# Splitting the node products of the second half into F32R parts, with three buffers in place of four

## The reference

```python
row, col = src, dst                      # edge_index[0], edge_index[1]
neighbor_sum = segment_sum(x[col], row)  # over the edges
deg = maximum(segment_sum(ones, row), 1)
mean_neighbor = neighbor_sum / deg[:, None]
h_mean = (x + mean_neighbor) * 0.5 @ W_mean + b_mean
h_concat = concatenate([x @ W_ego + b_ego, mean_neighbor @ W_nb + b_nb], axis=1)
gate = sigmoid(gate_weight * node_vec + gate_bias)[:, None]
x = layernorm(x + (1 - gate) * h_mean + gate * h_concat)
```

## Time and profile before

| | |
|---|---|
| median of 3 runs | 2863.28 us (2862.87 to 2864.31) |
| profiled execution, its own time | 2864.34 us |
| its span in the trace | 2862.5 us |
| mean granted TensorE clock | 0.973 of full speed |
| PE busy in the span | 2641.2 us (92%) |
| DVE / ACT / POOL busy | 2393.4 (84%) / 1851.0 (65%) / 1582.5 (55%) us |

### The profile page before, as it was taken

One profiled execution on the slowest core, in us unless ns is written; L12 is line 12 of the kernel. 1 busy time (PEld: TensorE's weight loads), 2 busy tenths in 40 slices (PEclk: granted clock), 3 DMA queues, 4 the chain that ended last, 5 costly groups with the idle time before them and its releaser, 6 DMA issues. The chain is left out here.

```text
span 2862.5 us, 53163 instructions
## 1 busy us (share of the span) xinstructions
PE 2641.2 (92%) x14009; PEld 1610.8 (56%) x14009; DVE 2393.4 (84%) x7769; ACT 1851.0 (65%) x3839; POOL 1582.5 (55%) x1491
## 2 busy tenths in 40 slices
PE   4699989999999499999999999999999999976774
PEld 2466668788887255555555555555555555543442
DVE  8888877777777688888888888888888888878996
ACT  2355555666665277777777777777777777757885
POOL 0476727777776555454545454545455555306776
PEclk9799999999999699999999999999999999989998
DMA  9899986666665587777777777777777777647894
GB/s 346 298 350 350 351 295 202 198 199 203 203 204 183 155 211 220 213 220 214 220 213 222 214 222 212 219 218 221 213 223 213 222 212 217 180 131 239 276 281 149
DMA packets 544668, 653.52 MB, mean 228 GB/s; under 512 B 244334, under 2 KB 451882, under 8 KB 544550
## 3 DMA queue, kind: packets, MB, share of 16 engines
q1 hardware_dynamic: 468518, 440.38, 52.2%
q0 software_dynamic: 69472, 208.99, 23.4%
q10 hardware_dynamic: 6560, 2.84, 0.4%
HBM read 315.65 MB, written 299.10 MB: 215 GB/s over the span
## 5 line engine op out<-in xcount | busy, mean ns | idle before, releaser
L1242 ACT ACTIVATE hidT<-bank,b1c 128x512 f32<-128x512 f32 x490 | 336.7, 687 | 414.3 <-PE bank L1532 340.4
L1151 POOL TENSOR_TENSOR u_hc<-u_hc 128x1536 f32<-128x1536 f32 x98 | 270.1, 2756 | 550.9 <-issue 429.4
L961 PE MATMUL bank<-w_node,xT 128*128 128x384 f32 x1564 | 558.6, 495 | 15.1 <-ACT bank L584 15.0
L1532 PE MATMUL bank<-xh,w1h 128*128 128x512 f16 x1568 | 469.2, 381 | 23.3 <-DMA xh<-eh 15.7
L1532 PE MATMUL bank<-xl,w1h 128*128 128x512 f16 x1568 | 468.2, 380 | 0.0
L1532 PE MATMUL bank<-xh,w1l 128*128 128x512 f16 x1568 | 468.2, 380 | 0.0
L584 ACT ACTIVATE bank<-bias_all 128x512 f32<-128x512 f32 x391 | 234.3, 599 | 235.7 <-DVE H L689 234.3
L961 PEld LDWEIGHTS bank<-w_node,xT 128*128 128x128 f32 x1564 | 288.5, 193 | 161.4 <-ACT bank L584 17.2
L1548 PE MATMUL bank<-hidT,w2f 128*64 128x256 f32 x3136 | 360.1, 382 | 0.8 <-ACT hidT L1242 0.8
L1373 DVE STREAM_TRANSPOSE feat<-catT 32x256 f32<-32x256 f32 x784 | 342.5, 437 | 17.0 <-ACT catT L1251 2.4
L1354 DVE TENSOR_SCALAR hidT<-bank,b1c 128x512 f32<-128x512 f32 x294 | 220.6, 750 | 120.7 <-PE bank L1532 112.3
(11 more groups left out here) (255 smaller groups left out, 5199.3 us busy)
## 6 DMA issues: line engine op xcount, KB each, us to landing
hc_tab<-H SPq DMA_DIRECT2D x78, 680.0 KB
er<-edge_tab SPq DMA_DIRECT2D x98, 512.0 KB, 4.4
X<-in_x SPq DMA_DIRECT2D x78, 640.0 KB, 5.2
h_row<-hc_tab SPq DMA_DIRECT2D x97, 512.0 KB
out_x<-o_row SPq DMA_DIRECT2D x97, 512.0 KB, 5.0
edge_tab<-u_x SPq DMA_DIRECT2D x98, 256.0 KB, 3.9
edge_tab<-feat SPq DMA_DIRECT2D x98, 256.0 KB
hc_tab<-zero_row SPq DMA_DIRECT2D x18, 1344.0 KB
```

The costliest lines, as they stand in the source:

```text
L961: ins = t_.matmul(p[:, 0:384], xT[t // 2 % XR][:, t % 2, c * P:(c + 1) * P], w_node[:, c, :], start=False, stop=c == 1, skip_group_check=True)
L1151: g.tensor_tensor(c, c, u_hc[s][:, :, MULT:MULT + 3].unsqueeze(3).to_broadcast([P, 4, 3, P]), ALU.mult).then_inc(u_scaled, 1)
L1242: a.activation(hidT[m][:, :], bank[2 + m % 2][:, :], ACT.Relu, bias=b1c[:, m:m + 1])\
L1532: ins = t_.matmul(bank[2 + m % 2][:, :], w[:, c, m * P:(m + 1) * P], xx[s][:, :, :].rearrange("p (k c) e -> p c k e", c=2)[:, c, :, :], st ...
```

## The change

From pair 92 (tile 184) on, a node pair is split as the edge sums are: ACT writes the rounded F32R copy to `xhigh`, DVE subtracts it from bank 0 into `xlow` (`low_x`, at odd steps, behind `add` and ahead of the other side work), and `product` issues six F32R matmuls with the split weights `w_nodeh`, `w_nodel`. PE's `turn` of the next pair then waits for `low_x`, not for ACT's copy. The buffers `xT` and `accT`/`accL` go from four to three; `xhigh` and `xlow` have three each. `DECODE` goes from step 16 to 20, the sums begin at step 184 and spread over 188 steps, and `PUT_LAG` goes from 13 to 29.

```diff
@@ weights
+        w_nodeh, w_nodel = sb("w_nodeh", [P, 2, 384], F32R), sb("w_nodel", [P, 2, 384], F32R)
...
                 st.done(v.tensor_copy(w_nbh[:, :, :], w_nb[:, :, :]))
-                st.wait()
+                st.done(v.tensor_copy(w_nodeh[:, :, :], w_node[:, :, :]))
+                st.wait()
+                st.done(v.tensor_tensor(w_nodel[:, :, :], w_node[:, :, :], w_nodeh[:, :, :].bitcast(F32),
+                                        ALU.subtract))
@@ buffers
-        XR = 4
+        XR = 3
         xT = [tmp(f"xT{b}", [P, 2, D]) for b in range(XR)]
+        XS = 3
+        xlow = [tmp(f"xlow{b}", [P, 2, D], F32R) for b in range(XS)]
+        xhigh = [tmp(f"xhigh{b}", [P, 2, D], F32R) for b in range(XS)]
+        x_low = sem("x_low")
...
-        AR = 4
+        AR = 3
@@ plan
-        PUT_LAG = 13
-        SORT, PHASES, DECODE, SUMS, SPAN, FIX = 0, 7, 16, 195, 177, 377
+        PUT_LAG = 29
+        SORT, PHASES, DECODE, SUMS, SPAN, FIX = 0, 7, 20, 184, 188, 377
+        SPLIT = SUMS // 2 // 1 * 1
+        SPLITS = tuple(range(SPLIT, NT // 2 + 1, 1))
+        def nth(p):
+            return (p - SPLIT) // 1
+        def in_parts(p):
+            return p in SPLITS
@@ ScalarE, copy_x
+                    to = xhigh[nth(p) % XS] if in_parts(p) else xT[p % XR]
@@ VectorE
+                def low_x(p):
+                    many = min(2, NT + 1 - 2 * p)
+                    dve.wait_ge(xt_copied, p + 1)
+                    if nth(p) >= XS:
+                        dve.wait_ge(p_ready, 2 * SPLITS[nth(p) - XS] + 2)
+                    q = nth(p) % XS
+                    v.tensor_tensor(xlow[q][:, 0:many, :],
+                                    bank[0][:, 0:many * D].rearrange("p (t d) -> p t d", t=many),
+                                    xhigh[q][:, 0:many, :].bitcast(F32), ALU.subtract).then_inc(x_low, 1)
...  in side(), behind decode, tables and shares, ahead of low_sum and run_sum
+                    if now % 2 == 1 and in_parts((now - 1 + LEAD_X) // 2):
+                        low_x((now - 1 + LEAD_X) // 2)
@@ TensorE, turn
-                    if p:
+                    if in_parts(p - 1):
+                        pe.wait_ge(x_low, nth(p - 1) + 1)
+                    elif p:
                         pe.wait_ge(xt_copied, p)
@@ TensorE, product
+                    pair = t // 2
+                    if in_parts(pair):
+                        pe.wait_ge(x_low, nth(pair) + 1)
+                        high, low = xhigh[nth(pair) % XS][:, t % 2, :], xlow[nth(pair) % XS][:, t % 2, :]
+                        n = 0
+                        for c in range(2):
+                            for part_, w in ((high, w_nodeh), (high, w_nodel), (low, w_nodeh)):
+                                n += 1
+                                ins = t_.matmul(p[:, 0:384], part_[:, c * P:(c + 1) * P], w[:, c, :], start=False,
+                                                stop=n == 6, skip_group_check=True)
+                        ins.then_inc(p_ready, 1)
+                        return
```

More of the change, by code:

```diff
@@ L575, in copy_x @@
                     many = min(2, NT + 1 - 2 * p)
-                    a.activation(xT[p % XR][:, 0:many, :], bank[0][:, 0:many * D].rearrange("p (t d) -> p t d", t=many),
+                    to = xhigh[nth(p) % XS] if in_parts(p) else xT[p % XR]
+                    a.activation(to[:, 0:many, :], bank[0][:, 0:many * D].rearrange("p (t d) -> p t d", t=many),
                                  ACT.Copy).then_inc(xt_copied, 1)
@@ L958, in product @@
                     p = bank[NODE[t % 3]]
-                    pe.wait_ge(xt_copied, t // 2 + 1)
+                    pair = t // 2
[10 more added lines that the diff above has]
+                        return
+                    pe.wait_ge(xt_copied, pair + 1)
                     for c in range(2):
```

## The result

| | before | after |
|---|---|---|
| median of 3 runs | 2863.28 us | 2893.21 us (2892.90 to 2893.98) |
| span of the profiled execution | 2862.5 us | 2892.2 us |
| mean granted TensorE clock | 0.973 | 0.972 |
| PE / DVE busy | 2641.2 / 2393.4 us | 2605.5 / 2450.4 us |

The changed kernel is slower: the ratio is 1.0101, with a 95% interval from 1.0087 to 1.0116. PE is busy 36 us less, and still the span is 29.7 us longer.

A forecast was written before the change was run, and what follows sets the result against it. TensorE was taken to set the pace at full clock, POOL nearly as full. Terms +15 + 4 - 6 + 1.5 + 7 = +21.5 us on 2864.34 gave 2885.8, forecast as 2885 us; range 2840 to 2902.

The forecast's parts named there:

- The wait: Before the next node turn, PE waits for low_x, queued on DVE behind the odd tile's three instructions: 1.21 us uncovered.
- One sign: Expected in the trace: POOL waits for acc in the blocks of steps where PE waits for low_x.
- 188 steps, +15: Node steps 185 to 372, with sums: 548 us where the same steps cost 533 before, so 15 us lost.
- Steps without sums, +4: Steps 181 to 184 and 375 to 390: same wait, two steps 3.84 instead of 3.02; 4 us lost, bounds 0 to 7.
- Decode, -6: Decode four steps later: four more tiles of 1.51 us fit into DVE's wait for the sorted edges; 6 us won.
- start, +1.5: Ahead of the stage: two more weight splits on DVE (0.56 and 0.96) with nothing beside them; 1.5 us lost.
- The start of the sums, +7: Steps 184 to 205: about 4 us waiting for first gathered rows, some 3 more at the cn ring; bounds 0 and 15.
- the POOL rival: Node stage: the wait is covered and POOL's gathers and scatters set the pace; about 2841 us, chance 0.15.
- Rings, 0: Three buffers in place of four in the rings of node pairs and sums cost nothing.
- A smaller wait: The turn's wait for low_x is near 0.8 us and cancels against the gain: 2855 to 2868 us, chance 0.14.
- The dearer hand-over: At step 205, clears drain slower beside earlier gathers and ACT stands 20 us longer: about 2905 us, chance 0.06.
- The clock rival: PE falls to half clock in steps with the uncovered wait: some 185 us more, 3070 us, chance 0.03.

The follow-up runs named there:

- the early clears: Table's last clears in two larger pieces behind tiles 184 and 189, not five: changed kernel 2875.09 us; kernel before with new decode, sums and lag, unsplit products, 2855.46 us.
- The plan alone: Kernel before with decode at step 20, sums from step 184 over 188 steps and put lag 29, products left in float32: 2868.78 us, ratio 1.0014.

## Why the prediction came out as it did

The sign and the mechanism were right, and one term of the sum was too small by more than half.

*The wait.* Forecast: about 1.2 us, some 50 times, released by DVE's write of `xlow`, in blocks set by the parity of the sums. The trace has exactly these blocks. Each link of the chain holds: DVE starts 0.20 behind the odd product (507.34 to 507.54), and from the end of that product's issue to L872 it is 1.94 us in the cycle shown, which is 1.31 without the gate copy (0.09) and the variances (0.54); 1.30 was forecast. The last link was shorter: L872 ends 0.06 ahead of the turn, where 0.15 was taken. There are 52 pauses in the whole stage, one of them the 7.58 at the start of the sums. The 43 of 470 to 930 us are 1.03 on average by the profile, which counts from the modelled end of a record, 0.34 behind its start where the next could have started after 0.175; with that difference 1.2. The run with `low_x` at the even step shows that it is this wait which costs: without it the time falls by 41 us. One sign came out only weakly: POOL was to wait for `acc` in the blocks, and from 470 to 930 us it waits 4.7 us for it, but 25.7 us for ACT's `cn`.

*188 steps, +15.* Two steps take 5.08 where 5.17 was forecast, and 6.33 on the mean of the five cycles from 497.12 to 528.75 where 6.29 was forecast. With these, 44 x 5.08 + 46 x 6.33 + 4 x 7.7 = 545.5 us, against 548 (the 7.7 is the forecast's own). The term stands at about +12.

*Steps without sums, +4.* The end of the stage has grown by 4.7 us. Of these 1.9 lie ahead of POOL's carry scatter, which waits 13.34 us for DVE where it waited 11.44; the other 2.8 lie between it and the next stage, and what makes them was not looked for. No run tested this term by itself. The split's three terms together (+15, +4 and +1.5 for the start, 20.5 in all) have a run: with the early clears, which take the stops for `cn` out of both sides, the split with its wait cost 19.6 us.

*Decode, -6 and start, +1.5.* Decode alone was -6.1. PE's first instruction of the node stage stands at 29.94, and stood at 28.60: +1.3.

*The start of the sums, +7 (bounds 0 and 15): the step that was mis-sized.* The first scatter was put at 428 (in the working of the POOL rival) and came at 437.54. The wait for the first gathered rows was put at 4 us; DVE waited 5.83, and PE, whose turn stands behind it in DVE's order, 7.58. Behind that stop PE ran at a granted clock of 0.50 (378 to 383 us), with records 0.32 us apart in place of 0.175; the forecast had no price for that, though its own show a product of 2.93 us behind a stop of 7.20 us, and the granted clock of before is 0.50 there as well (110 to 113 us). The last clear went out at 426.98, 16.0 later than before, where the forecast allowed 7.6 for clear and scatter together. Then the `cn` ring, as forecast, stopped PE, but for 11.34 and 3.81 us in place of some 3 more than DVE's 9.06 before. Subtracting the other terms from the measured loss, 29.9 + 6.1 - 1.3 - 12 - 4.7, leaves 18 us for this term; with the 19.6 that the runs give for the split, 29.9 + 6.1 - 19.6, it is 16.4. Both are a little above its upper bound, and both are remainders. The plan alone shows 10 of it with unsplit products; the 6 on top come only with the split, where PE stops 15.2 us for `cn` in place of 9.9 and 7.58 for the first gathered rows in place of 5.95. An earlier clear gives 20 us back in after, which includes some of the wait that the kernel before had there already. No other term of the sum was off by more than 3 us, as far as the marks and runs separate them.

*Rings, 0.* No run tests the rings of three by themselves. The view of waits of after has no wait for `xhigh`, `xlow`, `accT` or `accL` that it puts down to the products which read them (L998, L1042).

*The rivals.* POOL as the bound with the wait covered was wrong for this kernel: POOL waits 3.9 to 4.5 us for `cn` between several of its last pairs of scatters. The rival's arithmetic holds all the same. With `low_x` at the even step that case comes true, and the line of 2.6 us from a first scatter at 436.75 ends at 911.37. A smaller wait was wrong: it was 1.2 us. The dearer hand-over came true in its effect, not by its reason: from the last clear's issue to the first scatter it took 10.6 us where it had taken 9.4, so the clears drained hardly slower; the last clear itself went out later. The clock rival was wrong: from 470 to 930 us, where PE waits 43 times for `low_x`, 44.4 us in all, its mean granted clock is 1.00, and from 600 to 700 us, with PE busy 88.90 of 100 us, it is 1.00 too.

## What to carry to other kernels

When an engine's buffer is released by one more instruction, ask where that instruction stands in the order of the engine that runs it: behind three instructions that need the next product it turned 50 us of saved matmul time into a loss of 20, and one step earlier the split gained 30. When the engine that sets the pace becomes faster, look up who is next (here POOL, at 77 of 100 us busy and with a gap of 0.30 us behind each instruction) and when that one may start; both had to be mended before the gain came through. A wait that is taken away is worth only what the next wait leaves: with `low_x` at the even step PE's wait for it fell from 60.8 to 0.5 us and the time by 41, and then POOL's unbroken line, 2.60 us for a gather and a scatter, set the end of the sums.

## What was not expected of the hardware

Behind each of the three long stops (7.58, 11.34 and 3.81 us) PE ran at half clock, a granted clock of 0.50, for 3 to 6 us. The forecast had half clock only as a rival for the short pauses. The windows of after behind the three stops (columns as in the earlier trace rows):

```profile
378.00:383.00 5.00, 4.89 (x20) 4.77 (x21) 3.75 (x10) 1.92 (x5) 3.78 (x5) 0.50 0.68 223
444.70:447.70 3.00, 2.98 (x9) 3.00 (x10) 0.96 (x4) 2.45 (x6) 2.25 (x3) 0.50 0.32 113
448.10:455.50 7.40, 7.40 (x49) 7.07 (x47) 6.96 (x23) 3.07 (x6) 5.88 (x6) 1.00 0.55 158
459.40:465.00 5.60, 5.59 (x18) 5.60 (x18) 2.94 (x7) 3.51 (x8) 4.08 (x6) 0.50 0.35 113
```

From 445.18 to 447.74 records of the same shape start 0.32 us apart, at a granted clock of 0.50. From 448.06 on the distance is 0.175, but for the first record behind each transpose (0.26), at 1.00. The pauses of 0.8 to 1.5 us in the blocks had no such effect: the windows from 600 to 700 and from 470 to 930 us stay at 1.00.
